# Tile 1's attention moved forward: its first half into the opening, its second half beside tile 0's outer products

## The reference

```
q, k = sigmoid(x Wq + bq), sigmoid(x Wk + bk);  v = x Wv + bv        (16 heads of 8)
sink_in = n / sum_d(q * cumsum(k));  src_out = n / sum_d(k * cumsum(q))      n = position
cons_sink = sum_d(q * cumsum(k * src_out)) / n;  cons_src = clip(sum_d(k * cumsum(q * sink_in)) / n)
e = exp(cons_src);  comp = e / cumsum(e) * n;  alloc = sigmoid(cons_sink)
kv = cumsum(outer(k, v * comp));  attn = (q * sink_in / n) . kv * alloc
h = norm(x + attn Wo + bo);  x1 = norm(h + gelu(h W1 + b1) W2 + b2);  x2 = norm(x + x1)
out = norm(x2 + sum over 8 experts of gate_e * (relu(x2 wi + bi + lora_e(x2)) wo + bo))
```

## Time and profile before

| | us |
|---|---|
| median of 3 runs (lowest to highest) | 418.44 (418.27 to 419.03) |
| the profiled execution's own time | 418.39 |
| its span | 416.6 |
| PE busy | 374.6 (90%) |
| DVE busy | 327.9 (79%) |
| POOL busy | 223.2 (54%) |
| ACT busy | 216.6 (52%) |

### The profile page before, as it was taken

One profiled execution on the slowest core, in us unless ns is written; L12 is line 12 of the kernel. 1 busy time (PEld: TensorE's weight loads), 2 busy tenths in 40 slices (PEclk: granted clock), 3 DMA queues, 4 the chain that ended last, 5 costly groups with the idle time before them and its releaser, 6 DMA issues.

```text
span 416.6 us, 6454 instructions
## 1 busy us (share of the span) xinstructions
PE 374.6 (90%) x2082; PEld 261.3 (63%) x2082; DVE 327.9 (79%) x787; ACT 216.6 (52%) x399; POOL 223.2 (54%) x263
## 2 busy tenths in 40 slices
PE   8897789788998999989998999899989997799991
PEld 3555556465756875677657774778478765775551
DVE  3649966599589988999799979997899889832632
ACT  2240226327853586538852795278644874175541
POOL 2017234983279527963497348942795369735211
PEclk9999999899999999999999999999999999999997
DMA  8236006400180007300560028000810063000000
GB/s 257 115 71 158 1 2 152 125 3 0 37 217 2 0 2 183 97 0 2 116 162 2 0 56 223 3 0 16 204 36 0 2 160 68 0 1 27 12 14 25
DMA packets 19857, 26.58 MB, mean 64 GB/s; under 512 B 1648, under 2 KB 9968, under 8 KB 19824
## 3 DMA queue, kind: packets, MB, share of 16 engines
q1 hardware_dynamic: 19680, 25.96, 24.5%
q10 hardware_dynamic: 144, 0.21, 0.3%
HBM read 7.29 MB, written 2.10 MB: 23 GB/s over the span
## 4 chain that ended last, share of the span: by engine, by line
PE 31%; DVE 27%; POOL 19%; issue 14%; DMA 5%; ACT 2%; SPq 0%; POOLq 0%; DVEq 0%; ACTq 0%
POOL prod L848 12%; PE pB L354 5%; DMA vb<-vs 5%; DVE kv L1037 5%; PE pY L428 4%; PE pG L421 3%; DVE cum_kv L1043 3%; DVE cum_ks L937 2%; PE pG L497 2%; POOL rstd L838 2%; PE pG L490 2%; DVE cum_q L937 2%; PE pY L508 2%; DVE cum_qs L937 2%; DVE gel L1141 2%
## 5 line engine op out<-in xcount | busy, mean ns | idle before, releaser
L848 POOL TENSOR_TENSOR prod<-cum_kv,q_fac 128x512 f32<-128x512 f32 x64 | 94.5, 1483 | 33.9 <-DVE cum_kv L1043 25.7
L404 PEld LDWEIGHTS pO<-s_wor,prod 128*128 128x128 f32 x512 | 62.2, 191 | 33.5 <-POOL prod L848 21.4
L404 PE MATMUL pO<-s_wor,prod 128*128 128x128 f32 x512 | 69.5, 281 | 14.0 <-POOL prod L848 13.9
L1037 DVE TENSOR_TENSOR kv<-k,vb 128x512 f32<-128x512 f32 x64 | 52.8, 825 | 6.7 <-DMA vb<-vs 6.7
L835 POOL TENSOR_TENSOR var_eps<-mv,s_con 128x4 f32<-128x4 f32 x32 | 9.9, 310 | 71.1 <-DVE mv L1063 71.1
L1043 DVE TENSOR_TENSOR_SCAN cum_kv<-p_ones,cum_kv,kv 128x512 f32<-128x512 f32 x32 | 40.5, 1275 | 0.6
L1043 DVE TENSOR_TENSOR_SCAN cum_kv<-p_ones,kv 128x512 f32<-128x512 f32 x32 | 38.5, 1213 | 0.5
L657 ACT ACTIVATE v<-pA,s_att 128x512 f32<-128x512 f32 x7 | 4.8, 687 | 62.9 <-PE pA L340 62.9
L754 ACT ACTIVATE relu<-pG,s_att 128x512 f32<-128x512 f32 x28 | 19.2, 684 | 27.4 <-PE pG L490 27.4
L508 PEld LDWEIGHTS pY<-s_moe,gel 128*128 128x128 f32 x256 | 30.7, 192 | 3.7 <-issue 1.9
L508 PE MATMUL pY<-s_moe,gel 128*128 128x128 f32 x256 | 32.6, 276 | 0.0
(11 more groups left out here) (164 smaller groups left out, 772.7 us busy)
## 6 DMA issues: line engine op xcount, KB each, us to landing
vb<-vs SPq DMA_DIRECT2D x64, 256.0 KB, 4.7
xT<-x_t SPq DMA_DIRECT2D x8, 256.0 KB, 4.3
xt<-x SPq DMA_DIRECT2D x8, 256.0 KB, 5.3
out<-y SPq DMA_DIRECT2D x8, 256.0 KB, 2.3
s_moe<-moe_w SPq DMA_DIRECT2D x1, 836.0 KB, 10.4
s_wor<-wo_rep SPq DMA_DIRECT2D x1, 512.0 KB, 8.2
s_ffn<-ffn_w SPq DMA_DIRECT2D x1, 512.0 KB, 8.9
s_con<-consts SPq DMA_DIRECT2D x1, 502.0 KB, 4.4
```

The lines of the kernel that those rows point to most:

```text
L404: mm = pe.matmul(pO3[:, s, :], prod[:, m % 4, s * P:(s + 1) * P], s_wor[:, m, :], start=False, stop=(m == DH - 1), skip_group_check=True)
L848: pool.tensor_tensor(prod[:, m % 4, :], cum_kv[t.par][:, m, :], q_fac[t.par][:, :], ALU.mult).then_inc(prod_ready, 1)
L1037: dve.tensor_tensor(kv[:, m % 3, :], k[t.par][:, :], vb[:, m, :], ALU.mult).then_inc(kv_ready, 1)
```

## The change

The first half of tile 1's attention (projections of q and k, running sums, kq and qk, head sums, reciprocals, their transposes, and v) is put into the opening of each engine. Tile 1's q projection goes to bank pG[1] and its k projection and first head sums to pM, since pA and pB are in use by tile 0. DVE gets an opening of its own. In second_step, tile 1's second half is put between tile 0's outer products, so that values and query_factor of tile 1 stand before moments of tile 0; the row r_cmoe moves behind them. On POOL e_normal of tile 1 moves from behind the products to the place before product 6. Fillers on PE are placed anew. Waits are added where a single buffer is now written earlier: kq and qk (first products of tile 1) wait for tile 0's second head sums, rden for tile 0's q_scale, rden_n and rden_x for tile 0's readers. SP's order is as it was.

```diff
@@ -191,6 +191,12 @@
         pO3, pY3, pM3 = (b[:, :].rearrange("p (s n) -> p s n", s=SUB) for b in (pO, pY, pM))
         res[0], res[1] = pO3, pY3
+        def q_bank(t):
+            return pG[1] if t.n == 1 else pA
+
+        def k_bank(t):
+            return pM if t.n == 1 else pB
+
         def v_bank(t):
             return pG[0] if t.n == 0 else pA
...
@@ -326,16 +335,20 @@
         def _(pe):
             def project_q(t):
                 pe.wait_ge(xT_loaded[t.par], 16 * (t.slot_uses + 1))
-                wait(pe, qfac_ready, t.n)
-                pe.matmul(pA[:, :], att("wq"), xT[t.par][:, :], start=True, stop=True).then_inc(q_proj, 1)
+                if t.n > 1:
+                    pe.wait_ge(qfac_ready, t.n)
+                pe.matmul(q_bank(t)[:, :], att("wq"), xT[t.par][:, :], start=True, stop=True).then_inc(q_proj, 1)
             def project_k(t):
                 pe.wait_ge(xT_loaded[t.par], 16 * (t.slot_uses + 1))
-                wait(pe, vs_ready, t.n)
-                pe.matmul(pB[:, :], att("wk"), xT[t.par][:, :], start=True, stop=True).then_inc(k_proj, 1)
+                if t.n > 1:
+                    pe.wait_ge(vs_ready, t.n)
+                pe.matmul(k_bank(t)[:, :], att("wk"), xT[t.par][:, :], start=True, stop=True).then_inc(k_proj, 1)
             def project_v(t):
-                if t.n > 0:
+                if t.n == 1:
+                    pe.wait_ge(qfac_ready, t.n)
+                elif t.n > 1:
                     pe.wait_ge(q_ready, t.n + 1)
                 pe.matmul(v_bank(t)[:, :], att("wv"), xT[t.par][:, :], start=True, stop=True).then_inc(v_proj, 1)
...
@@ -370,6 +384,7 @@
                     pe.wait_ge((v_ready if t.n > 0 else q_ready), t.n + 1)
                 else:
                     pe.wait_ge(k_ready, t.n + 1)
+                    wait(pe, vs_ready, t.n)
                 spread_T((pA, pB)[i], rden_x[:, i, :, :].rearrange("p a b -> p (a b)"), (sinkT_ready, srcT_ready)[i])
             def factor_T(t):
...
@@ -529,50 +544,54 @@
             def opening(a):
+                b = a.plus(1)
                 project_q(a); project_k(a); project_v(a)
-                keep_busy(1)
                 pe.matmul(pO[:, :], onesrow[:, 0:P], onesrow[:, :], start=True, stop=True).then_inc(po_written, 1)
+                project_q(b); project_k(b)
                 head_sums(a, 0, True); head_sums(a, 0, False)
                 keep_busy(2)
                 denominators_T(a, 0); denominators_T(a, 1)
                 keep_busy(3)
                 head_sums(a, 1, True); head_sums(a, 1, False)
                 keep_busy(1)
+                head_sums(b, 0, True)
                 cumulate_e(a)
-                keep_busy(2)
+                head_sums(b, 0, False)
+                keep_busy(1)
                 compensation_T(a); factor_T(a)
+                keep_busy(3)
+                project_v(b)
+                denominators_T(b, 0); denominators_T(b, 1)
                 constant_row()
-                project_q(a.plus(1)); project_k(a.plus(1))
-                keep_busy(4)
                 pe.wait_ge(y_free[0], 16)
                 reduce_out(a, 0)
             def second_step(b):
                 a = b.plus(1)
+                keep_busy(1)
+                reduce_out(b, 1); reduce_out(b, 2)
+                keep_busy(1)
+                head_sums(a, 1, True)
+                reduce_out(b, 3)
+                keep_busy(1)
+                head_sums(a, 1, False)
+                reduce_out(b, 4)
                 keep_busy(2)
-                for m in range(1, 5):
-                    reduce_out(b, m)
-                head_sums(a, 0, True); head_sums(a, 0, False); project_v(a)
-                keep_busy(1)
                 reduce_out(b, 5)
-                denominators_T(a, 0); denominators_T(a, 1)
+                cumulate_e(a)
                 keep_busy(1)
                 reduce_out(b, 6)
-                head_sums(a, 1, True)
-                keep_busy(1)
-                head_sums(a, 1, False)
+                compensation_T(a); factor_T(a)
                 keep_busy(1)
                 reduce_out(b, 7)
                 keep_busy(2)
-                cumulate_e(a)
-                keep_busy(2)
-                h_T(b); compensation_T(a); factor_T(a)
+                h_T(b)
                 for f in range(FC):
                     hidden(b, f)
                 for f in range(FC):
                     ffn_out(b, f)
-                keep_busy(3, pM)
+                keep_busy(3, pG[1])
                 reduce_out(a, 0)
             def closing(c):
...
@@ -659,6 +678,7 @@
             def spread_denominators(t, i):
                 act.wait_ge(rdenn_ready, t.n + 1)
+                wait(act, (facT_ready, compT_ready)[i], t.n)
                 act.activation(rden_x[:, i, :, :], rden_n[:, i * HW:(i + 1) * HW].unsqueeze(2).to_broadcast([P, HW, DH]),
                                ACT.Copy).then_inc(rdenx_ready, 1)
...
@@ -760,20 +780,21 @@
             def opening(a):
-                q_out(a); k_out(a)
-                spread_denominators(a, 0); spread_denominators(a, 1); v_out(a)
+                b = a.plus(1)
+                q_out(a); k_out(a); v_out(a)
+                q_out(b); k_out(b)
+                spread_denominators(a, 0); spread_denominators(a, 1)
                 source_exp(a); alloc_tanh(a); allocation(a)
                 spread_scale(a, False); spread_scale(a, True)
-                q_out(a.plus(1)); k_out(a.plus(1))
                 seed_x(a)
+                spread_denominators(b, 0); spread_denominators(b, 1); v_out(b)
             def second_step(b):
                 a = b.plus(1)
-                v_out(a); spread_denominators(a, 0); spread_denominators(a, 1)
                 source_exp(a); alloc_tanh(a); allocation(a)
+                spread_scale(a, False); spread_scale(a, True)
                 normalise(b, 0)
-                spread_scale(a, False); spread_scale(a, True)
                 h_out(b)
                 gelu(b, 0); gelu(b, 1)
                 seed_h(b)
...
@@ -904,9 +925,11 @@
             def second_step(b):
                 a = b.plus(1)
-                for m in range(1, DH):
+                for m in range(1, 6):
                     product(b, m)
-                inverse_std(b, 0); e_normal(a); scaled_h(b); h_residual(b); attention_input(a)
+                e_normal(a)
+                product(b, 6); product(b, 7)
+                inverse_std(b, 0); scaled_h(b); h_residual(b); attention_input(a)
                 shifted_x(b); inverse_std(b, 1); product(a, 0); scaled_n2(b)
             def step(s):
...
@@ -954,6 +979,7 @@
                 dve.wait_ge((cumq_ready, cumqs_ready)[pair], t.n + 1)
                 dve.wait_ge(k_ready, t.n + 1)
+                wait(dve, (consp_ready, den_ready)[pair], 2 * (t.n + pair))
                 dve.scalar_tensor_tensor(kq[:, :], k[t.par][:, :], ATT_EPS, (cum_q, cum_qs)[pair][t.par][:, :],
                                          ALU.add, ALU.mult).then_inc((kq1_ready, kq2_ready)[pair], 1)
...
                 dve.wait_ge(den_ready, 2 * (t.n + 1))
-                dve.reciprocal(rden[:, :], p_den).then_inc(rden_ready, 1)
+                wait(dve, qscale_ready, t.n)
+                dve.reciprocal(rden[:, :], p_den(t)).then_inc(rden_ready, 1)
             def normal_denominators(t):
                 dve.wait_ge(rden_ready, t.n + 1)
                 if t.n == 0:
                     dve.wait_ge(con_loaded, 16)
                 at = t.par * 2 * HW
+                wait(dve, rdenx_ready, 2 * t.n)
                 dve.tensor_tensor(rden_n[:, :], rden[:, :], con("norm")[:, at:at + 2 * HW], ALU.mult).then_inc(rdenn_ready, 1)
             def sink(t):
...
@@ -1173,25 +1206,45 @@
                     second_relu(c, f)
                 expert_residual(c); moments(c, 3)
+            def opening(a):
+
+                b = a.plus(1)
+                cumulate_q(a); cumulate_k(a); k_times_cum_q(a, 0); q_times_cum_k(a, 0)
+                inverse_denominators(a); normal_denominators(a)
+                cumulate_q(b)
+                sink(a); cumulate_sink(a); source(a); k_times_cum_q(a, 1); cumulate_source(a); q_times_cum_k(a, 1)
+                cumulate_k(b)
+                k_times_cum_q(b, 0)
+                conserved(a); clip_source(a)
+                q_times_cum_k(b, 0)
+                prefix_e(a)
+                inverse_cum_e(a); source_factor(a); sink_factor(a)
+                values(a); query_factor(a)
+                inverse_denominators(b); normal_denominators(b)
+                outer_product(a, 0); cumulate_kv(a, 0); outer_product(a, 1)
+
             def second_step(b):
                 a = b.plus(1)
+                outer_product(b, 2); cumulate_kv(b, 1)
+                sink(a); cumulate_sink(a)
+                cumulate_kv(b, 2)
+                source(a); k_times_cum_q(a, 1); cumulate_source(a)
+                outer_product(b, 3); cumulate_kv(b, 3); outer_product(b, 4)
+                q_times_cum_k(a, 1)
```

(28 more changed lines are left out.)

12 lines of the change are left out of this document (10 added, 2 removed).

## The result

The changed kernel takes 422.31 us (median of 4 runs, 421.88 to 423.05) against 418.36 for the kernel before on the same chip: ratio 1.0089, 95% interval 1.0073 to 1.0105, slower by 3.9 us. The forecast was slower, 419.5, with a range up to 421.4.

A forecast was written before the change was run, and what follows sets the result against it. Bound mixed: DVE until moments(0,0), then tile 0's own line. Lateness 1.25 us less 0.20 slack gives 1.05; 418.39 + 1.05 = 419.44, said as 419.5, with 416.8 to 421.4 for 8 in 10.

The forecast's parts named there:

- The opening: Tile 0's attention, with tile 1's first half added: vs(0) and the first outer product come later, sum 0.94 us.
- PE's two projections: Opening, PE: tile 1's two projections, replacing one filler ahead of the head sums, delay those sums by 0.14 us.
- The second step: Tile 0's outer products beside tile 1's attention: replay puts moments(0,0) at 58.85 against 57.61, lateness 1.25 us.
- The four larger waits: Second step, DVE: kq, qk and prefix_e held by POOL's products, conserved by PE's head sums; 0.7, 1.1, 1.1, 0.7 us.
- clip and factors: Second step, DVE: the clip waits 0.3 us for product 4, and the factors are held 0.5 us.
- rival (2): Second step: port costs little, moments(0,0) at 56.25 and the 0.20 slack gone too; 416.8 us, chance 0.17.
- rival (1): No measurable change: the replay's errors cancel the 1.05 us; 417.6 to 418.9 us, chance 0.22.
- From moments(0,0) to the FFN the order is as before: Stretch after the second step: order unchanged; ACT's dropped scale spread worth 0 to 0.3 us, taken as 0.
- Rival (4): Second step, 42 to 45.5 us: PE's waiting halves its clock, conserved comes 1.9 us later; 421.4 us, chance 0.14.
- the replay: Second step, DVE's operations timed one by one in the new order: scan 7 comes 1.2 us later, moments(0,0) at 58.85.
- Rival (3): After the second step: tile 1's lead of 7 us is used whole; 411.4 us, chance 0.04.
- nothing gained: After the second step: values(1) comes 7.1 us earlier, but DVE then waits at moments(0,1), so no time is gained.

The follow-up runs named there:

- the run with the second step's order: Changed kernel plus four more fillers before h_T, with source(1), q_times_cum_k(1) and PE's second head sums moved earlier in the second step: 418.3 us, ratio 0.9989.

## Why the prediction was wrong

*The opening.* For DVE 0.80 us was forecast and 0.78 measured after the first reciprocal. Right, by its own steps: cons came 0.71 later after the first reciprocal (9.66 us against 8.95), where 0.60 was said. For PE's two projections 0.14 was forecast. From tile 0's first kq to the first reciprocal it is 2.87 us before and 3.12 after, but 2.93 to 3.31 in the other profiles with the new opening, so this term is only bounded.

*The second step.* Forecast 32.45 from values(0) to moments(0,0) (26.4 to 58.85), measured 32.12. The four larger waits were there at their size (kq 0.7, qk 1.1, cons 0.7, prefix_e 1.1); clip and factors were put at 0.8 and cost 0.2, which makes up more than the 0.3 between the two. So rival (2), which lived on doubts about the port, fell, and rival (1) with it: with the gap filled the ratio is still 1.0046. The run with the second step's order shows how near they were: with source, qk and the second head sums elsewhere this stretch is 1.73 us shorter, and the time is that of the kernel before. One reading of the port was too narrow: the clip was counted among the operations with both inputs in SBUF, and it has one. It did wait in the kernel before (0.95 us) and in the run with the second step's order (0.94). The 3.5 us of two scans and two products are 3.6 by their rows (39.47 to 43.07); nothing hangs on it.

*After it: the step that failed.* "From moments(0,0) to the FFN the order is as before" was taken for all engines. DVE, ACT and POOL only lost work of tile 1 there. PE lost what had kept it busy: cumulate_e and two pairs of fillers had stood between reduction 7 and h_T and filled the wait for n1; the change put cumulate_e ahead and left two fillers. The term for this stretch was nothing. Measured: 10.37 instead of 7.82 us from the hidden layer to moments(0,1), 2.55 us, shown both ways by the runs with the fillers added and taken away. The hidden layer alone lost 2.71; the difference is the slack of 0.20 before moments(0,1), nearly used up.

Ahead of the hidden layer 0.31 us more were measured where 0 was taken. POOL's shift came 0.48 later after moments(0,0), rstd having taken 1.50 instead of 1.02 beside the outer product, and 0.17 came back between h_T and hT, where ACT no longer had the scale spread. Both were named; they did not cancel. In sum, with the start left out: 0.27 to the first reciprocal, 0.78, -0.01, 0.31, 2.55 and twice 0.04 behind it are 4.0 us, the 3.95 of the medians. Without the 2.55 it would have been 1.4, near the forecast's 1.05.

*Rival (4)* had the mechanism, with its 2.38 us of waiting in the kernel before as the model, and put it at the wrong gap. The dip at 42 us came as described and cost nothing, since PE was ahead of POOL there. I looked for idle time where DVE needed PE, and not behind moments(0,0), where I had called everything unchanged. The range lacked its price for the FFN: half the clock on most of 4.05 us of matmuls. That the sign came out right is to the credit of the replay; the size was not forecast by any part of it.

*The lead.* Rival (3) was right to be small for this change, and "nothing gained" right as far as it went; up to 3.6 us of it can be had, by four engines' orders and not by the move alone, and with the third step's clock in these 3.6.

## What to carry to other kernels

When work moves from one engine's queue to an earlier place, list what it leaves behind in that queue: on PE the hole it had filled can cost more than the move gains, because what runs next may run at half clock (here 2.7 us on a hidden layer of 4.05). Check each gap ahead of a stage of long matmuls that is on the path; a dip over work that waits anyway is free, as the one at 42 us was. A wait of one engine for another's SBUF access is a matter of order: put two-input operations of DVE just ahead of the scan that releases POOL, and hand work into an idle stretch only as far as its contended length (here 1.67 for 0.67 us) fits.

## What the runs showed of the hardware

TensorE's clock fell to 0.50 without one long idle time. Ahead of the dip at 42 us PE was busy 1.15, 1.05, 0.94 and 1.14 us of four stretches of 2 us from 34 to 42, with no wait longer than 1.92; in the kernel before it did not fall after 1.22 and 1.16 of 2 us at 48 to 52. Under the dip the hidden layer took 5.25, 6.01 and 6.76 us in three kernels with waits of 2.4 to 3.5 us ahead of h_T.

DVE's scan prefix_e, with two SBUF inputs, waits for POOL like the elementwise operations (1.35 against 0.28). A scan that reads the ones from PSUM did not: cum_qs took 1.28 us at 37.07 beside the product that began at 36.46, and the same form took 1.28 at 14.62, with POOL idle. The clip of 64 columns, with one SBUF input, took 0.95 and 0.94 us beside a product and 0.19 in the opening with POOL idle; why an operation with one such input waits was not tested.
